# Context tail of a perceiver block: compact key-value matrices, attention in 32x64 tiles, two correction groups, last Gram split by column block

## Chip, cores, metric
The kernel runs on one core of one Trainium2 chip. The metric is the device time of one execution in microseconds (us), as the median of several executions. All data is 32-bit floating point at the borders of the kernel. An engine name below is one of TensorE (PE), VectorE (DVE), ScalarE (ACT), GpSimd (POOL) and SyncE (SP), which issues the transfers.

## What is computed
The reference is one perceiver layer: a linear cross attention to a context of 1601 rows for each of 8 batches, then a self attention and a gated mixture of experts. The change touches only the end of the first part:

```python
q = (decoder_seq @ Wq.T + bq).reshape(B, T_dec, N_HEADS, D_HEAD)   # 8, 64, 16, 32
k = (encoder_seq @ Wk.T + bk).reshape(B, T_enc, N_HEADS, D_HEAD)   # 8, 1601, 16, 32
v = (encoder_seq @ Wv.T + bv).reshape(B, T_enc, N_HEADS, D_HEAD)
kv = jnp.einsum('bthd,bthe->bhde', k, v)
att = jnp.einsum('bqhd,bhde->bqhe', q, kv) * scale
...
return layer_norm(att + decoder_seq, ln_gamma, ln_beta)
...
x = x + _L0_xattn_ref(ctx_1024, _layernorm(x, axis=-1), ...)
x = x + _L0_attn_ref(_layernorm(x, axis=-1), ...)
```

## The kernel before
There is no softmax in the cross attention, so each batch b needs only the Gram matrix G of its context (512x512), and from it one 32x32 matrix per head: KV = Wk G Wv^T, plus corrections of rank one for the two biases. The work is written out by hand, engine by engine, with semaphores between the engines; every engine runs its own list strictly in the order of the code.

For each batch TensorE sums the Gram matrix (`gram`, lines 936 to 960). Then `m_part(b, m)` makes block row m (128 rows) of M = G Wv^T in three products of halves (helper `three`, lines 367 to 369, 12 matmuls for each m), which ScalarE copies out (`m_copy`, line 656), and `kv_part(b)` (line 1008) makes the 16 head blocks. For the products G is held as a rounded part `gh` (made by ScalarE) and a remainder `gl` (made by VectorE).

The stretch that the change touches begins when the last Gram matrix (batch 7) is summed. There remain the M and KV of batch 6, the M and KV of batch 7, the corrections for batches 0 to 6, the attention of four tiles of 128 rows (two batches each), and the layer norms. In this stretch
- `group_corrections(n)` (lines 1093 and 1099) adds the bias terms to a group of batches: it copies their compact KV (128x128 each) into a PSUM bank by a product with the identity and adds 16 small products. The right operands are masked copies that ScalarE makes (`right_part`, line 716).
- `group_spread(n)` brings a group back to SBUF, spread from the compact 128 columns to a block-diagonal 128x512 matrix (VectorE line 1685, ScalarE line 734).
- `attend(i)` (line 1121) multiplies the queries of tile i with these matrices, in tiles of 128x64 of the array, into one bank.
- `part1_out(i)` (line 1700 and the four after it), `part1_residual(i)` (line 1714) and `norm_back(2, i)` (line 1473) on VectorE add the query's input to it, take two layer norms and give the rows `xn` of tile i. `transposes_1(i)` (line 1149) turns them on TensorE, and `xT_pair_high` and `xT_pair_low` (lines 755 and 1722) split them for `project_1`, the first product of the second part (lines 367 to 369, at 128x256).
- `kv_spread(7)` (line 1571) stands on VectorE behind `norm_back(2, 2)`; `attend(3)` waits for it, and `project_1` stands right behind `attend(3)`.
- `w_high(W_Q1)` on ScalarE (line 704) and `w_low(W_Q1)` on VectorE (line 1660) split the weight that `project_1` uses; the second waits for the first.
- `last_gh_high` and `last_gl_low` split the last Gram matrix, whose lower blocks still lie in PSUM after `last_g_transposes` (line 980).

```python
            group_spread(0)
            last_gl_low()
            part1_out(0)
            part1_residual(0)
            part1_out(1)
            norm_back(2, 0)
            part1_residual(1)
            part1_out(2)
            norm_back(2, 1)
            part1_residual(2)
            norm_back(2, 2)
            dve.wait_ge(xb_done, NT)
            kv_spread(B - 1)
            xT_pair_low(1, 0, range(KC))
            part1_out(3)
```

Of the kernel before, what the change touches and what calls it, by code (L numbers as in the profile page):

```python
# [34 lines left out]
def perceiver_block(nc, a, out):  # L35
# [25 lines left out]
    with ExitStack() as ctx:  # L61
# [230 lines left out]
        def att_bank(i):  # L292

            return bank[(5, 0, 3, 7)[i]]

# [17 lines left out]

        groups = ((0, 2), (2, 4), (4, 7))

        def group_bank(n):

            return bank[(1, 2, 4)[n]][:, 0:P * (groups[n][1] - groups[n][0])]

# [53 lines left out]
        def _(sp):  # L373
# [219 lines left out]
        def _(act):  # L593
# [116 lines left out]
            m_copy(B - 2, (1,))  # L710
            w_high(W_Q1, 0, 1)
            m_copy(B - 2, (2,))

# [3 lines left out]

            def last_gh_high():
                act.wait_ge(m_mm, (B - 1) * 4)
                act.wait_ge(gl_done, B - 1)  # L720
                act.wait_ge(g_add, 6 * B)
                act.activation(upper(ghf, 5 * P), upper(g32f, 5 * P), ACT.Copy).then_inc(gh_done, 1)
                act.activation(last_block(ghf), last_block(g32f), ACT.Copy).then_inc(gh_done, 1)
                act.wait_ge(gt_mm, 1)
                act.activation(lower(ghf), mir[:, 0:2, :].rearrange("p m n -> p (m n)")[:, 0:6 * P].rearrange("p (m n) -> p m n", m=3),
                               ACT.Copy).then_inc(gh_done, 1)

            def group_spread(n):

                act.wait_ge(r2_mm, n + 1)  # L730
                src = group_bank(n).rearrange("p (m d) -> p m d", d=D1)
                dst = kv[:, groups[n][0]:groups[n][1], :].rearrange("p b (c j d) -> p (b c) j d", j=4, d=D1)
                for j in range(4):
                    act.activation(dst[:, :, j, :], src, ACT.Copy, scale=headmask[:, D1 * j:D1 * j + 1]).then_inc(r2_act, 1)
# [12 lines left out]
            right_part(B - 1)  # L747
            m_copy(B - 1, (1,))
            w_high(W_OUT, 1, 1)
# [102 lines left out]
        def _(pe):  # L852
# [130 lines left out]
            def m_part(b, m, first):  # L983

                if first and m == 0:
                    pe.wait_ge(w_lo, 2)
                    pe.wait_ge(q_done, KC)
                if m == 0:
                    pe.wait_ge(gl_done, b + 1 if not isinstance(b, int) or b < B - 1 else B + 2)
                if not first and m == 0:  # L990
                    pe.wait_ge(kv_done, b)
# [8 lines left out]
            def kv_part(b, cs=range(KC)):  # L1000

                if cs.start == 0:
                    pe.wait_ge(m_done, b * 4 + 4)
                for c in cs:
                    for k in range(KC):
                        for j in range(4):
                            cols = slice(c * P + D1 * j, c * P + D1 * j + D1)
                            mm = pe.matmul(head_block(bank[6], c, j), wk[:, k, cols], mb[:, k, cols],  # L1008
                                           start=(k == 0), stop=(k == KC - 1))
                if cs.stop == KC:  # L1010
                    mm.then_inc(kv_mm, 1)

# [36 lines left out]
            with pe.Fori(2, B - 1) as b:  # L1049
                gram(b, False, lambda: kv_part(b - 2))  # L1050
                products_of(b - 1, False)
            gram(B - 1, False, lambda: kv_part(B - 3))

# [30 lines left out]
            def group_corrections(n):  # L1084

                first, end = groups[n]
                if n == 0:
                    pe.wait_ge(bk_near, 1)
                    pe.wait_ge(rk_near, 1)
                if n == 2:  # L1090
                    pe.wait_ge(gl_done, B + 2)
                pe.wait_ge(kv_done, end)
# [10 lines left out]
            def attend(i):  # L1103

                if i == 0:
                    pe.wait_ge(mir_mm, 1)
                    pe.wait_ge(g_add, 6 * B)
                if i == 1:
                    pe.wait_ge(rk_near, 1)
                    pe.wait_ge(right_near, 1)  # L1110
                if i == 0:
                    pe.wait_ge(r2_dve, 2)
                elif i < NT - 1:
                    pe.wait_ge(r2_act, 4 * i)
                else:
                    pe.wait_ge(kv_done, B)
                for c in range(KC):
                    for b in (2 * i, 2 * i + 1):
                        cols = slice(c * P, (c + 1) * P)
                        p0 = S * (b % 2)  # L1120
                        mm = pe.matmul(att_bank(i)[p0:p0 + S, cols], qT[:, c, b * S:(b + 1) * S], kv[:, b, cols],  # L1121
                                       start=True, stop=True)
                mm.then_inc(att_mm, 1)
# [52 lines left out]

            for m in range(2, KC):
                m_part(B - 1, m, False)
            last_kv_part()
# [279 lines left out]
        def _(dve):  # L1459
# [220 lines left out]
            def group_spread(n):  # L1680

                dve.wait_ge(r2_mm, n + 1)
                for b in range(groups[n][0], groups[n][1]):
                    m = b - groups[n][0]
                    dve.tensor_tensor(by_head_of(kv[:, b, :]), spread_heads(group_bank(n)[:, m * P:(m + 1) * P]), near_heads,
                                      ALU.mult).then_inc(r2_dve, 1)

            def last_gl_low():
                dve.wait_ge(gh_done, B + 1)
                dve.tensor_tensor(upper(glf, 5 * P), upper(g32f, 5 * P), upper(ghf, 5 * P).bitcast(F32), ALU.subtract).then_inc(gl_done, 1)  # L1690
                dve.tensor_tensor(last_block(glf), last_block(g32f), last_block(ghf).bitcast(F32), ALU.subtract).then_inc(gl_done, 1)
                dve.wait_ge(gh_done, B + 2)
                dve.tensor_tensor(lower(glf), mir[:, 0:2, :].rearrange("p m n -> p (m n)")[:, 0:6 * P].rearrange("p (m n) -> p m n", m=3),
                                  lower(ghf).bitcast(F32), ALU.subtract).then_inc(gl_done, 1)
# [29 lines left out]

            group_spread(0)
            last_gl_low()
            part1_out(0)
# [262 lines left out]
```

## Time and profile before
| | |
|---|---|
| median of 3 executions | 561.12 us (561.01 to 561.72) |
| profiled execution | 561.45 us, span 559.7 us |
| mean granted clock of TensorE | 0.997 of full speed |
| busy: PE, DVE, ACT, POOL | 546.4, 377.6, 283.6, 245.8 us |

The span runs from the first to the last instruction. A timeline row gives the start of an instruction (or of several alike, with their count), its duration, its engine and line, what it writes and reads, its shape, and in brackets how long the engine had been idle before it and what ended that. Matmuls overlap in the engine's pipeline, so the time that a block of them takes is read from its first start to the start of the next block. One fp32 matmul of the code is two in the trace.

### The profile page before, as it was taken

To read this page: it belongs to the slowest core of one execution; us is meant where nothing else is said; L and a number is where in the kernel's file an instruction comes from. 1 tells how busy PE (TensorE), PEld (TensorE's weight loads), DVE (VectorE), ACT (ScalarE), POOL (GpSimd) and SP (SyncE) were. 2 spreads that over 40 slices of the span, in tenths; PEclk is the share of its full clock that TensorE was granted. 3 is DMA by queue.
4 is the path that set the end of the run, shared out by engine and by line. 5 is a ranking of instruction groups with operands and counts; after the bars stand their busy time and mean duration, and the time that the engine had idled before them with its cause. 6 is when DMAs were issued, how large, how long until landed. Compare 5 with 4: busy or idle time off the path is not lost.

```text
span 559.7 us, 11752 instructions
## 1 busy us (share of the span) xinstructions
PE 546.4 (98%) x4873; PEld 466.9 (83%) x4875; DVE 377.6 (67%) x482; ACT 283.6 (51%) x486; POOL 245.8 (44%) x182
## 2 busy tenths in 40 slices
PE   9999969999999999999899999999999999999997
PEld 7988759898988989897679998978788888888886
DVE  4899488695977868684597477476584457867731
ACT  4687764886949496872742543424331213434220
POOL 2297989776766769677025001103345443000000
PEclk9999989999999999999999999999999999999999
DMA  8742562523432332305640004207733222899502
GB/s 309 255 142 82 211 188 77 185 77 114 148 101 94 133 123 75 114 1 185 165 171 4 10 8 147 76 2 189 198 122 105 75 81 81 207 249 212 150 0 76
DMA packets 31414, 69.13 MB, mean 123 GB/s; under 512 B 6928, under 2 KB 6928, under 8 KB 28432
## 3 DMA queue, kind: packets, MB, share of 16 engines
q1 hardware_dynamic: 31376, 68.58, 40.4%
q8 instruction: 29, 0.48, 0.4%
q14 instruction: 9, 0.07, 0.0%
HBM read 67.39 MB, written 1.18 MB: 123 GB/s over the span
## 4 chain that ended last, share of the span: by engine, by line
PE 84%; DVE 2%; issue 1%; POOL 1%; ACT 0%; POOLq 0%
PE ps L367 18%; PE ps L369 17%; PE ps L368 17%; PE ps L936 8%; PE ps L956 3%; PE ps L960 3%; PE ps L952 2%; PE ps L947 2%; PE ps L946 2%; PE ps L951 2%; PE ps L1008 2%; PE ps L1245 1%; PE ps L1228 1%; PE ps L1121 1%; PE ps L1158 1%
## 5 line engine op out<-in xcount | busy, mean ns | idle before, releaser
L533 POOL TENSOR_TENSOR psum_tmp<-psum_tmp,raw 128x512 f32<-128x512 f32 (+1 forms) x86 | 157.3, 1829 | 26.9 <-DVE lo L1491 18.6
L936 PE MATMUL ps<-hi 128*128 128x256 f32 (+1 forms) x384 | 120.6, 316 | 6.4 <-DVE lo L1491 6.4
L936 PEld LDWEIGHTS ps<-hi 128*128 128x128 f32 x384 | 73.2, 191 | 8.7 <-issue 5.7
L367 PE MATMUL ps<-hi,gh 128*128 128x512 f32 x192 | 75.5, 393 | 0.0
L369 PE MATMUL ps<-hi,gl 128*128 128x512 f32 x192 | 74.8, 390 | 0.0
L368 PE MATMUL ps<-lo,gh 128*128 128x512 f32 x192 | 74.7, 389 | 0.0
L586 POOL TENSOR_TENSOR sx<-sx,raw 128x512 f32<-128x512 f32 x32 | 41.1, 1291 | 76.4 <-DVE raw L1883 76.2
L631 ACT ACTIVATE kv<-par 32x320 f32<-32x320 f32 x112 | 52.7, 470 | 40.3 <-DVE par L1539 39.0
L823 ACT ACTIVATE hi<-raw 128x2048 fp32r<-128x2048 f32 x14 | 26.9, 1918 | 88.6 <-PE ps L369 79.3
L1491 DVE TENSOR_TENSOR lo<-raw,hi 128x2048 fp32r<-128x2048 f32 (+1 forms) x28 | 70.1, 2503 | 0.3
L367 PE MATMUL ps<-wvh,gh 128*128 128x512 f32 x128 | 50.9, 398 | 0.0
L369 PE MATMUL ps<-wvh,gl 128*128 128x512 f32 x128 | 49.9, 390 | 0.0
L368 PE MATMUL ps<-wvl,gh 128*128 128x512 f32 x128 | 49.9, 390 | 0.0
L511 POOL TENSOR_TENSOR rstd<-vareps,expo 128x1 f32<-128x1 f32 x16 | 11.1, 695 | 84.1 <-DVE vareps L1467 84.1
L607 ACT ACTIVATE hi<-raw 128x2048 fp32r<-128x2048 f32 (+1 forms) x28 | 42.7, 1540 | 10.2 <-DMA raw<-in_ctx 10.0
L1889 DVE TENSOR_TENSOR lo<-raw,hi 128x2048 fp32r<-128x2048 f32 x15 | 34.4, 2291 | 18.0 <-ACT hi L823 17.9
L369 PEld LDWEIGHTS ps<-hi,gl 128*128 128x128 f32 x192 | 36.0, 188 | 7.5
L640 ACT ACTIVATE g<-par 32x192 f32<-32x192 f32 x112 | 40.6, 363 | 3.3 <-DVE par L1558 2.1
L367 PEld LDWEIGHTS ps<-hi,gh 128*128 128x128 f32 x192 | 36.0, 188 | 7.5
L368 PEld LDWEIGHTS ps<-lo,gh 128*128 128x128 f32 x192 | 36.1, 188 | 7.3
L956 PE MATMUL ps<-lo,hi 128*128 128x512 f32 x104 | 41.5, 399 | 0.0
L960 PE MATMUL ps<-lo,hi 128*128 128x512 f32 x104 | 41.2, 396 | 0.0
(231 smaller groups left out, 1187.9 us busy)
## 6 DMA issues: line engine op xcount, KB each, us to landing
raw<-in_ctx SPq DMA_DIRECT2D x22, 1024.0 KB, 5.3
raw<-in_ve SPq DMA_DIRECT2D x8, 1024.0 KB, 6.1
raw<-in_oe SPq DMA_DIRECT2D x8, 1024.0 KB, 6.6
wk<-gm_rows SPq DMA_DIRECT2D x8, 512.0 KB, 9.2
g<-gm_rows SPq DMA_DIRECT2D x8, 512.0 KB, 10.8
raw<-in_ctx SPq DMA_DIRECT2D x16, 128.0 KB, 4.2
cb<-in_ctx SPq DMA_DIRECT2D x8, 256.0 KB, 3.2
xres<-in_x SPq DMA_DIRECT2D x1, 1024.0 KB, 9.6
```

The source lines that it names most:

```text
L367: pe.matmul(dst, wh, xh, start=first, stop=False)
L368: pe.matmul(dst, wh, xl, start=False, stop=False)
L369: return pe.matmul(dst, wl, xh, start=False, stop=last)
L533: pool.tensor_tensor(psum_tmp[0:k, :], psum_tmp[0:k, :] if n else rows(order[0]), rows(t)[0:k, :], ALU.add).then_inc(ctx_sum, 1)
L586: pool.tensor_tensor(v, v, tmp[:, i % 2, :].rearrange("p (h k) -> p h k", k=D2), ALU.add).then_inc(v_added, 1)
L607: act.activation(hi[:, r, :], ctx_rows(b, c), ACT.Copy).then_inc(ctx_hi, 1)
L631: ins = act.activation(turned[dst, :, :, src], flipped[src, :, dst].rearrange("p (r s) n -> p r s n", s=2), ACT.Copy)
L640: ins = act.activation(low_pairs(dst)[:, :, :, src], upflip[src, :, :, dst], ACT.Copy)
L936: pe.matmul(dst, hi[:, t, cols], x, start=start and opens, stop=t == CH * ROWS - 1 and closes, skip_group_check=True)
L956: pe.matmul(mir[:, 0, :], w, lb, start=start, stop=stop, skip_group_check=True)
L960: mm = pe.matmul(mir[:, 1, :], w, lb, start=start, stop=stop, skip_group_check=True)
L1491: dve.tensor_tensor(lo[rows, r, :], ctx_rows(b, c)[rows, :, :], hi[rows, r, :].bitcast(F32), ALU.subtract).then_inc(ctx_lo, 1)
```

## The change
The key-value matrices of batches 0 to 5 stay compact. The corrections are made for two groups (batches 0 to 3 and 4 to 6) in place of three. Tiles 0 to 2 are attended head by head in tiles of 32x64 of the array, into four banks, one for each row group. The lower blocks of the last Gram matrix are first copied to SBUF, and its `gh` and `gl` are then made by column block, four pieces each. The program order changes with it on TensorE, ScalarE and VectorE: `last_g_transposes` and `m_part(7, 0)` come before the corrections, `attend(0)` and `attend(1)` stand together behind `kv_part(6)`, and the two steps that split W_Q1 come later.

```diff
-            return bank[(5, 0, 3, 7)[i]]
+            return bank[7] if i == NT - 1 else ps[:, 2:6, i * P:(i + 1) * P].rearrange("p j (c d) -> p c j d", d=D1)
+
+        def kv_bank(b):
+
+            return bank[0][:, 3 * P:4 * P] if isinstance(b, int) and b == B - 2 else bank[6][:, 0:P]
...
-        groups = ((0, 2), (2, 4), (4, 7))
+        groups = ((0, 4), (4, 7))
...
-            sp.wait_ge(r2_mm, 2)
+            sp.wait_ge(r2_mm, 1)
             sp.dma_start(raw[:, half(1), :], blocks(a["owT"])).then_inc(ld_w[1], 16)
-            sp.wait_ge(gl_done, B + 2)
+            sp.wait_ge(gl_done, B + 3)
             sp.dma_start(g32[:, :, :], blocks(a["vw"])).then_inc(ld_qv, 16)
...
@@ ScalarE
             m_copy(B - 2, (1,))
-            w_high(W_Q1, 0, 1)
-            m_copy(B - 2, (2,))
...
+            def last_lower_blocks():
+                act.wait_ge(gt_mm, 1)
+                act.activation(lower(g32f), mir[:, 0:2, :].rearrange("p m n -> p (m n)")[:, 0:6 * P].rearrange("p (m n) -> p m n", m=3),
+                               ACT.Copy).then_inc(lower_done, 1)
+
+            def last_gh_high(m):
+                act.wait_ge(m_mm, (B - 2) * 4 + m + 1)
...
+                act.activation(gh[:, :, of_tile(m)], g32[:, :, of_tile(m)], ACT.Copy).then_inc(gh_done, 1)
...
+            last_lower_blocks()
+            last_gh_high(0)
+            last_gh_high(1)
+            m_copy(B - 2, (2,))
             for b in range(4):
                 right_part(b)
             m_copy(B - 2, (3,))
-            last_gh_high()
-            group_spread(1)
+            last_gh_high(2)
+            last_gh_high(3)
             act.wait_ge(kv_mm, B - 1)
-            act.activation(kv[:, B - 2, 0:P], bank[6][:, 0:P], ACT.Copy).then_inc(kv_done, 1)
+            act.activation(kv[:, B - 2, 0:P], kv_bank(B - 2), ACT.Copy).then_inc(kv_done, 1)
+            m_copy(B - 1, (0,))
             for b in range(4, 7):
                 right_part(b)
-            m_copy(B - 1, (0,))
-            group_spread(2)
+            w_high(W_Q1, 0, 1)
+            m_copy(B - 1, (1,))
+            group_copy(1)
             right_part(B - 1)
-            m_copy(B - 1, (1,))
             w_high(W_OUT, 1, 1)
...
@@ TensorE
             def attend(i):
 
                 if i == 0:
-                    pe.wait_ge(mir_mm, 1)
-                    pe.wait_ge(g_add, 6 * B)
...
+                    pe.wait_ge(lower_done, B)
+                    pe.wait_ge(r2_dve, 1)
+                if i == 2:
+                    pe.wait_ge(r2_act, 1)
+                    pe.wait_ge(y_done, 2)
+                if i == NT - 1:
+                    pe.wait_ge(r2_act, 5)
                     pe.wait_ge(kv_done, B)
...
+                        for j in range(4):
+                            row = slice(D1 * j, D1 * j + D1)
+                            mm = pe.matmul(att_bank(i)[p0:p0 + S, c, j, :], qT[row, c, b * S:(b + 1) * S], kv[row, b, D1 * c:D1 * c + D1],
+                                           start=True, stop=True, skip_group_check=True)
...
             sum_rows()
+            last_g_transposes()
             m_part(B - 2, 2, False)
             m_part(B - 2, 3, False)
+            m_part(B - 1, 0, False)
             group_corrections(0)
-            last_g_transposes()
+            kv_part(B - 2, kv_bank(B - 2))
+            attend(0)
+            attend(1)
+            m_part(B - 1, 1, False)
             group_corrections(1)
-            kv_part(B - 2)
-            attend(0)
-            m_part(B - 1, 0, False)
-            attend(1)
-            group_corrections(2)
-            m_part(B - 1, 1, False)
+            m_part(B - 1, 2, False)
             attend(2)
+            m_part(B - 1, 3, False)
 
             def transposes_1(i):
 
+                if i == 0:
+                    pe.wait_ge(y_done, NT - 1)
                 pe.wait_ge(s_norm[2], i + 1)
...
@@ VectorE
-            w_low(W_Q1, 0)
...
             def part1_out(i):
 
                 dve.wait_ge(s_norm[0], i + 1)
-                dve.wait_ge(att_mm, i + 1)
-                dve.tensor_tensor(xn[:, i, :], xn[:, i, :], att_bank(i)[:, :], ALU.add).then_inc(y_done, 1)
+                dve.wait_ge(att_mm, max(i + 1, 2))
+                dve.tensor_tensor(by_head_of(xn[:, i, :]), by_head_of(xn[:, i, :]), att_bank(i) if i < NT - 1 else by_head_of(att_bank(i)),
+                                  ALU.add).then_inc(y_done, 1)
...
-            group_spread(0)
-            last_gl_low()
+            for m in range(KC):
+                last_gl_low(m)
+            group_copy(0)
+            w_low(W_Q1, 0)
             part1_out(0)
```

Three places show how the lists of the engines differ. The line numbers of the changed kernel are 4 to 13 higher for the same code. First ScalarE, before, from the split of W_Q1 (line 704, reads `raw`, writes `hi`) to the right operands of batches 4 to 6; `mb` is a copy of M, `gh` the rounded Gram matrix:

```order
L704 ACTIVATE hi<-raw 128x2048 [waits ld_w0]
L656 ACTIVATE mb<-ps 128x512 [waits m_mm]
L716 ACTIVATE raw<-raw,batch_of 128x512 [waits right_near] x4
L656 ACTIVATE mb<-ps 128x512 [waits m_mm]
L722 ACTIVATE gh<-g 128x3x384 [waits g_add,gl_done,m_mm]
L723 ACTIVATE gh<-g 128x128
L725 ACTIVATE gh<-ps 128x3x256 [waits gt_mm]
L734 ACTIVATE kv<-ps,headmask 128x8x32 [waits r2_mm]
L734 ACTIVATE kv<-ps,headmask 128x8x32 x3
L742 ACTIVATE kv<-ps 128x128 [waits kv_mm]
L716 ACTIVATE raw<-raw,batch_of 128x512 [waits right_near] x3
```

The same stretch of the changed kernel, where the split of W_Q1 is line 708:

```order
L722 ACTIVATE g<-ps 128x3x256 [waits gt_mm]
L730 ACTIVATE gh<-g 128x4x128 [waits g_add,lower_done,gl_done,m_mm] x2
L660 ACTIVATE mb<-ps 128x512 [waits m_mm]
L718 ACTIVATE raw<-raw,batch_of 128x512 [waits right_near] x4
L660 ACTIVATE mb<-ps 128x512 [waits m_mm]
L730 ACTIVATE gh<-g 128x4x128 [waits g_add,lower_done,gl_done,m_mm] x2
L752 ACTIVATE kv<-ps 128x128 [waits kv_mm]
L660 ACTIVATE mb<-ps 128x512 [waits m_mm]
L718 ACTIVATE raw<-raw,batch_of 128x512 [waits right_near] x3
L708 ACTIVATE hi<-raw 128x2048 [waits ld_w0]
```

The split of W_Q1 has moved from the head of the list to its end, behind the copy of KV of batch 6 (which waits for `kv_mm`), a copy of M and three right operands.

Second VectorE, before, from the last mask of the right operands (line 1677) to the first instruction of `part1_out(0)` (line 1700):

```order
L1677 TENSOR_TENSOR raw<-raw,hm 128x512 [waits pick_done,rv_sum]
L1660 TENSOR_TENSOR lo<-raw,hi 128x2048 [waits w_hi]
L1685 TENSOR_TENSOR kv<-ps,headmask 128x512 [waits r2_mm]
L1685 TENSOR_TENSOR kv<-ps,headmask 128x512
L1690 TENSOR_TENSOR gl<-g,gh 128x3x384 [waits gh_done]
L1691 TENSOR_TENSOR gl<-g,gh 128x128
L1693 TENSOR_TENSOR gl<-ps,gh 128x3x256 [waits gh_done]
L1700 TENSOR_TENSOR xn<-xn,ps 128x512 [waits att_mm,s_norm0]
```

And in the changed kernel, where these are lines 1690 and 1705, and the remainder of W_Q1 is line 1673:

```order
L1690 TENSOR_TENSOR raw<-raw,hm 128x512 [waits pick_done,rv_sum]
L1699 TENSOR_TENSOR gl<-g,gh 128x4x128 [waits gh_done] x4
L1695 COPY kv<-ps 128x4x128 [waits r2_mm]
L1673 TENSOR_TENSOR lo<-raw,hi 128x2048 [waits w_hi]
L1705 TENSOR_TENSOR xn<-xn,ps 128x512 [waits att_mm,s_norm0]
```

The remainder of W_Q1, which waits for ScalarE's half, now stands directly ahead of `part1_out(0)`.

Third TensorE, before, from the corrections of the first group (line 1093) to `attend(0)` (line 1121); line 980 is `last_g_transposes`, line 1008 `kv_part(6)`:

```order
L1093 MATMUL ps<-kv,ident 128x256 [waits kv_done,rk_near,bk_near]
L1099 MATMUL ps<-raw 32x2x32 [waits rb_done]
L1099 MATMUL ps<-raw 32x2x32 x15
L980 MATMUL ps<-ident,g 128x128 [waits g_add]
L980 MATMUL ps<-ident,g 128x128 x5
L1093 MATMUL ps<-kv,ident 128x256 [waits kv_done]
...
L1008 MATMUL ps<-mb,wk 32x32 [waits m_done]
L1008 MATMUL ps<-mb,wk 32x32 x63
L1121 MATMUL ps<-kv,qT 64x128 [waits r2_dve,g_add,mir_mm]
L1121 MATMUL ps<-kv,qT 64x128 x7
```

In the changed kernel, from the transposes (line 991, now ahead of `m_part(6, 2)`) to the two attended tiles; the row of line 371 with `gl_done` opens `m_part(7, 0)`:

```order
L991 MATMUL ps<-ident,g 128x128 [waits g_add]
...
L371 MATMUL ps<-wvh,gh 128x512 [waits m_done,gl_done]
...
L1102 MATMUL ps<-kv,ident 128x512 [waits kv_done,rk_near,bk_near]
L1108 MATMUL ps<-raw 32x4x32 [waits rb_done]
L1108 MATMUL ps<-raw 32x4x32 x15
L1020 MATMUL ps<-mb,wk 32x32 [waits m_done]
L1020 MATMUL ps<-mb,wk 32x32 x63
L1133 MATMUL ps<-kv,qT 64x32 [waits r2_dve,lower_done]
L1133 MATMUL ps<-kv,qT 64x32 x63
```

`kv_part(6)` stands behind `m_part(7, 0)` and one larger group of corrections, and the 64 matmuls of tiles 0 and 1 follow it.

## Rows read from the trace of the kernel before

**Rows 1.** The page, part 1: busy time of each engine over the span.
```profile
PE 546.4 (98%) x4873; PEld 466.9 (83%) x4875; DVE 377.6 (67%) x482; ACT 283.6 (51%) x486; POOL 245.8 (44%) x182
```

**Rows 2.** Timeline of TensorE, from sum_rows to project_1.
```profile
267.13 0.50 PE L367 MATMUL ps<-wvh,gh 128*128 128x512 f32 x1
...
270.03 0.39 PE L367 MATMUL ps<-wvh,gh 128*128 128x512 f32 x1
...
272.76 0.60 PE L1093 MATMUL ps<-kv,ident 128*128 128x256 f32 x2
...
273.87 0.87 PE L980 MATMUL ps<-ident,g 128*128 128x128 f32 x6
274.58 0.60 PE L1093 MATMUL ps<-kv,ident 128*128 128x256 f32 x2
...
275.58 1.30 PE L1008 MATMUL ps<-mb,wk 128*32 128x32 f32 x128
276.81 0.76 PE L1121 MATMUL ps<-kv,qT 128*64 128x128 f32 x9
279.08 0.66 PE L1121 MATMUL ps<-kv,qT 128*64 128x128 f32 x7 [1.51 <-issue]
...
283.65 0.91 PE L1093 MATMUL ps<-kv,ident 128*128 128x384 f32 x2
...
285.29 0.50 PE L367 MATMUL ps<-wvh,gh 128*128 128x512 f32 x1
...
296.48 1.09 PE L1149 MATMUL ps<-ident,xn 128*128 128x128 f32 x8
297.51 1.09 PE L1121 MATMUL ps<-kv,qT 128*64 128x128 f32 x16
298.53 0.39 PE L367 MATMUL ps<-gh,hi 128*128 128x256 f32 x1
```

**Rows 3.** Timeline of ScalarE, same stretch.
```profile
265.39 0.60 ACT L656 ACTIVATE mb<-ps 128x512 f32<-128x512 f32 x1 [3.50 <-PE ps L369]
265.88 1.90 ACT L704 ACTIVATE hi<-raw 128x2048 fp32r<-128x2048 f32 x1
...
277.27 0.29 ACT L742 ACTIVATE kv<-ps 128x128 f32<-128x128 f32 x1
277.43 1.97 ACT L716 ACTIVATE raw<-raw,batch_of 128x512 f32<-128x512 f32 x3
```

**Rows 4.** Timeline of VectorE, same stretch.
```profile
269.32 2.29 DVE L1660 TENSOR_TENSOR lo<-raw,hi 128x2048 fp32r<-128x2048 f32 x1
...
279.85 0.69 DVE L1700 TENSOR_TENSOR xn<-xn,ps 128x512 f32<-128x512 f32 x1 [2.22 <-PE ps L1121]
...
284.62 0.69 DVE L1700 TENSOR_TENSOR xn<-xn,ps 128x512 f32<-128x512 f32 x1
...
289.45 0.69 DVE L1700 TENSOR_TENSOR xn<-xn,ps 128x512 f32<-128x512 f32 x1
...
291.84 0.54 DVE L1473 TENSOR_SCALAR xn<-xres,mv,rstd 128x512 f32<-128x512 f32 x1
...
295.01 1.51 DVE L1473 TENSOR_SCALAR xn<-xres,mv,rstd 128x512 f32<-128x512 f32 x1 [0.66 <-POOL rstd L511]
296.66 0.69 DVE L1571 TENSOR_TENSOR kv<-ps,headmask 128x512 f32<-128x512 f32 x1
297.70 1.42 DVE L1722 TENSOR_TENSOR gl<-ps,gh 128x256 fp32r<-128x256 f32 x4 [0.35 <-ACT gh L755]
```

**Rows 5.** Timeline of TensorE where it idled longest.
```profile
75.07 0.68 PE L936 MATMUL ps<-hi 128*128 128x384 f32 x1 [5.26 <-DVE lo L1491]
```

**Rows 6.** Windows there; after busy times: granted clock, DMA share, GB/s.
```profile
74.50:75.00 0.50, 0.00 (x0) 0.00 (x0) 0.50 (x2) 0.00 (x0) 0.50 (x1) 0.67 0.71 270
...
78.00:78.50 0.50, 0.50 (x41) 0.36 (x43) 0.50 (x2) 0.50 (x2) 0.34 (x2) 0.91 0.00 0
```

**Rows 7.** Timeline of TensorE, products in 32x64 tiles of the second part.
```profile
314.01 1.63 PE L1214 MATMUL ps<-qT 32*64 32x64 f32 x128
```

More of the change, by code:

```diff
@@ L312, in right_of @@
             return raw[:, 4 + b, :] if b < B - 1 else psum_tmp[:, :]
-        groups = ((0, 2), (2, 4), (4, 7))
+        groups = ((0, 4), (4, 7))
         def group_bank(n):
-            return bank[(1, 2, 4)[n]][:, 0:P * (groups[n][1] - groups[n][0])]
+            return bank[(1, 0)[n]][:, 0:P * (groups[n][1] - groups[n][0])]
         def by_tile(t):
@@ L987, in m_part @@
                     pe.wait_ge(q_done, KC)
[L988 to L991, printed above, removed]
+                if isinstance(b, int) and b == B - 1:
+                    pe.wait_ge(gl_done, B + m)
+                elif m == 0:
+                    pe.wait_ge(gl_done, b + 1)
+                    if not first:
+                        pe.wait_ge(kv_done, b)
                 if not (first and m < 2):
@@ L998, in m_part, with kv_part @@
                 mm.then_inc(m_mm, 1)
[L1000 to L1004, printed above, removed]
+            def kv_part(b, dst):
+                pe.wait_ge(m_done, b * 4 + 4)
+                for c in range(KC):
                     for k in range(KC):
@@ L1007, in kv_part @@
                             cols = slice(c * P + D1 * j, c * P + D1 * j + D1)
[L1008 to L1011, printed above, removed]
+                            mm = pe.matmul(head_block(dst, c, j), wk[:, k, cols], mb[:, k, cols],
+                                           start=(k == 0), stop=(k == KC - 1), skip_group_check=True)
+                mm.then_inc(kv_mm, 1)
             def last_kv_part():
@@ L1049, in _ @@
             with pe.Fori(2, B - 1) as b:
-                gram(b, False, lambda: kv_part(b - 2))
+                gram(b, False, lambda: kv_part(b - 2, bank[6]))
                 products_of(b - 1, False)
-            gram(B - 1, False, lambda: kv_part(B - 3))
+            gram(B - 1, False, lambda: kv_part(B - 3, bank[6]))
             def row_sums():
@@ L1089, in group_corrections @@
                     pe.wait_ge(rk_near, 1)
-                if n == 2:
-                    pe.wait_ge(gl_done, B + 2)
                 pe.wait_ge(kv_done, end)
@@ L1120, in attend @@
                         p0 = S * (b % 2)
-                        mm = pe.matmul(att_bank(i)[p0:p0 + S, cols], qT[:, c, b * S:(b + 1) * S], kv[:, b, cols],
-                                       start=True, stop=True)
+                        if i == NT - 1:
+                            mm = pe.matmul(att_bank(i)[p0:p0 + S, cols], qT[:, c, b * S:(b + 1) * S], kv[:, b, cols],
+                                           start=True, stop=True)
+                            continue
+                        for j in range(4):
+                            row = slice(D1 * j, D1 * j + D1)
+                            mm = pe.matmul(att_bank(i)[p0:p0 + S, c, j, :], qT[row, c, b * S:(b + 1) * S], kv[row, b, D1 * c:D1 * c + D1],
+                                           start=True, stop=True, skip_group_check=True)
                 mm.then_inc(att_mm, 1)
@@ L1175, in project_1 @@
                         mm.then_inc(q_mm, 1)
-            for m in range(2, KC):
-                m_part(B - 1, m, False)
             last_kv_part()
@@ L1677, in _, with group_copy, last_gl_low @@
             dve.tensor_tensor(by_tile(right), by_tile(right), near4(slice(0, P)), ALU.mult).then_inc(right_near, 1)
-            w_low(W_Q1, 0)
-            def group_spread(n):
+            def group_copy(n):
                 dve.wait_ge(r2_mm, n + 1)
[L1683 to L1694, printed above, removed]
+                dve.tensor_copy(kv[:, groups[n][0]:groups[n][1], 0:P], group_bank(n).rearrange("p (m d) -> p m d", d=P)).then_inc(r2_dve, 1)
+            def last_gl_low(m):
+                dve.wait_ge(gh_done, B + m)
+                dve.tensor_tensor(gl[:, :, of_tile(m)], g32[:, :, of_tile(m)], gh[:, :, of_tile(m)].bitcast(F32), ALU.subtract).then_inc(gl_done, 1)
             def part1_out(i):
                 dve.wait_ge(s_norm[0], i + 1)
-                dve.wait_ge(att_mm, i + 1)
-                dve.tensor_tensor(xn[:, i, :], xn[:, i, :], att_bank(i)[:, :], ALU.add).then_inc(y_done, 1)
+                dve.wait_ge(att_mm, max(i + 1, 2))
+                dve.tensor_tensor(by_head_of(xn[:, i, :]), by_head_of(xn[:, i, :]), att_bank(i) if i < NT - 1 else by_head_of(att_bank(i)),
+                                  ALU.add).then_inc(y_done, 1)
                 dve.wait_ge(y_done, i + 1)
```

26 lines of the change are left out of this document (7 added, 19 removed).

## Prediction
> **What bounds the kernel now.** I read the page's busy times first: TensorE is busy for 546.4 of 559.7 us [rows 1], so a change pays only where it takes work or waits off TensorE, and costs wherever it makes TensorE wait. Then its timeline in the touched stretch: one gap of 1.51 us stands out, in the middle of `attend(0)`, with no other engine as its releaser [rows 2]. Then the timelines of the three engines side by side from 267 to 299 us. TensorE has no other gap there: `project_1` starts at 298.53, straight behind `attend(3)` (297.51), which follows the transposes (296.48) [rows 2]. The reader should see how narrow that is. VectorE starts `part1_out(0)` at 279.85, has `part1_out(1)` and `(2)` at 284.62 and 289.45, `norm_back(2, 1)` at 291.84, and `kv_spread(7)` from 296.66 to 297.35, 0.16 us before `attend(3)` [rows 4]. Of these 17.5 us the largest idle time is 0.66, for one of GpSimd's small powers ahead of 295.01; the list is dense. So two chains end together at `project_1`: TensorE's work, and VectorE's list from `part1_out(0)` on. The start of `part1_out(0)` decides for the second; I call it T0, now 279.85.
>
> **TensorE's own sum.** Attention of a tile takes 1.02 us (297.51 to 298.53, 16 matmuls in the trace) [rows 2]. After, tiles 0 to 2 have 64 each, of 32 columns in 32x64 tiles. No row has just this; the nearest is 128 of 64 columns in the same tiles in 1.63 us, 12.7 ns each [rows 7], which gives 0.81 us as the upper bound; 128 of 32 columns in 128x32 tiles start in 1.23 us (275.58 to 276.81) [rows 2], 9.6 ns each, which gives 0.61. I take 0.7: 3 x 0.3 = 0.9 us less. Corrections: a group of two takes 1.11 us (272.76 to 273.87) or 1.00 (274.58 to 275.58), one of three 1.64 (283.65 to 285.29) [rows 2]. One batch more costs 0.53, so a group of four takes 2.17; together 3.75 before, 3.81 after, no gain. The gap of 1.51 may go or stay. So TensorE alone would gain 0.9 to 2.4 us. On ScalarE and VectorE the spreads become cheaper copies and the Gram pieces stay as large in sum; both lie before T0 and beside matmuls, so they count only through T0.
>
> **T0 after the change.** Step by step from 267.13, where TensorE has finished `sum_rows` in either kernel (nothing ahead of it is changed on its path):
> - `last_g_transposes` 0.71 (273.87 to 274.58), `m_part(6, 2)` 2.90 and `m_part(6, 3)` 2.73 (267.13, 270.03, 272.76), `m_part(7, 0)` 2.73 more, corrections of the group of four 2.17, `kv_part(6)` 1.23 [rows 2]. That is 12.47, so `kv_mm` comes at 279.6, or 279.65 with the end of the last matmul, against 276.9 before. `m_part(7, 0)` starts at 273.5 and needs only the first column block of `gh` and `gl`. From the transposes at 267.84, ScalarE copies 768 and 512 columns (under the 1.90 of 2048) [rows 3] and VectorE makes a remainder of 512 (under 2.29) [rows 4]: done by 272.0 at the latest, so `m_part(6, 2)` and `(6, 3)` cover it; without them `m_part(7, 0)` would wait up to 4.2 us.
> - ScalarE stands at its copy of KV of batch 6 and waits for it. Behind it: the copy itself 0.16 to the next start (277.27 to 277.43), a copy of M 0.49 (265.39 to 265.88), three right operands 1.9 (of 1.97), then `w_high(W_Q1)` 1.90 [rows 3]. Sum 4.45: done at 284.1. Before, this last step ended at 267.8, under `sum_rows`.
> - VectorE has nothing to do between its copy of the group (278.4 + at most 0.69, 279.1) and this. `w_low(W_Q1)` takes 2.29 [rows 4]. T0 = 286.4.
> - `part1_out(0)` also waits for tiles 0 and 1: 279.6 + 2 x 0.7 = 281.0, or 282.5 with a gap as now. That is covered by 4 us or more.
>
> So T0 moves from 279.85 to 286.4, by 6.55 us. That is the main term. Queued behind the waiting `w_low` are all of `part1_out`, `part1_residual`, `norm_back`, `kv_spread(7)` and `xT_pair_low`; GpSimd's small powers wait with them.
>
> **What TensorE does with it.** It has the work up to `attend(2)` done at about 281.0 + 2.9 + 1.64 + 2.8 = 288.3 (289.8 with the gap). The copy of the second group on ScalarE, needed by then, comes after `w_high(W_Q1)` and `m_copy(7, 1)`, at about 286, in time. But `attend(2)` now waits for `y_done` 2, which is T0 + 5.46 (284.62 + 0.69 - 279.85) [rows 4] = 291.9: a new wait of 2 to 3.5 us. Behind it stand `m_part(7, 3)`, the last KV product and the transposes. They end about 297.2. `transposes_1(0)` needs `y_done` 3, T0 + 10.3 = 296.7, no wait; `transposes_1(1)` needs `norm_back(2, 1)`, T0 + 12.5 = 298.9, a wait of 1.2. They end at 299.5. `attend(3)` needs `kv_spread(7)`, T0 + 17.5 = 303.9: a wait of 4.4. Then 1.02, and `project_1` starts at 304.95 where it started at 298.53, 6.4 us later. `xT_pair_low` no longer waits for ScalarE (0.35 before) [rows 4] and gives nothing more, for TensorE waits at `attend(3)`. All that TensorE saved in its own work lies ahead of these waits and is lost in them. Behind `project_1` TensorE has no slack to give it back [rows 1]. The loads are not in the way: owT is issued at the end of the first corrections (278.4), 2.8 us later than now and used at 287; wq2 is issued at T0, and its split comes after the second part's first products.
>
> **Sum.** 559.7 + 6.4 = 566.1 us of span. The profiled execution took 561.45 with this span, 0.33 above the median, which is 0.06%. On the median: 561.12 + 6.4 = 567.5.
>
> **The clock.** TensorE idled for 5.26 us before 75.07 [rows 5], and its granted clock, full until then, went to half (2.4 to 1.2 GHz) at about 74.7, some 5 us into the idle stretch, and came back near 78.05 [rows 6]. So 3.0 us of work ran at half speed and cost 1.5 us. The gap of 1.51 us cost none. The new wait of 4.4 us, with another of 1.2 and two short blocks of transposes ahead of it, lies between these, nearer to the first. If the clock falls in it, about 1.5 us is lost in `project_1`, which is TensorE's own work. If it falls in the wait ahead of `attend(2)`, the loss lies in the slack and costs nothing. The Trainium skill, "TensorE: Matmul & The Clock Gate", Part 1, states that an idle array is put back to half its clock and regains it only after sustained work; the row at 75.07 agrees, and by that rule the sum would be 6.4 + 1.5 = 7.9.
>
> **Rivals.**
> - *Clock falls as well*: 6.4 + 1.5, 569.0 us. For it the row at 74.5, against it that 4.4 is less than 5.
> - *The gap in issue comes ahead of `kv_mm`.* The gap stands behind a dense run: 128 matmuls in 1.23 us. After, the dense run is longer (128 and then 128). Counted in matmuls from the loop's end, the place of the present gap falls in the first quarter of the new attention, behind `kv_mm`, where 4 us cover it. If it fell inside `kv_part(6)`, T0 moves by 1.5 more: 569.0. The Trainium skill, "Runtime: NRT & Kernel Launch", Instruction fetch mechanics, calls the crossing of an instruction block mostly hidden; the 1.51 us above is a gap without another engine as releaser, and by that rule no term changes.
> - *VectorE's late start costs less*: the wait of 0.66 for GpSimd shrinks, or the group of four takes only 1.64 and the copies are quicker. Floor: T0 cannot be before tiles 0 and 1 are attended, 281.0, which is +1.2 us. Between: 562.3 to 566.
> - *Faster*: TensorE's own sum decides, 0.9 to 2.4 us less, 558.7 to 560.2. The place is `attend(3)`: it would need `kv_spread(7)` done no later than about 297, so T0 at 279.6 or earlier, or a list of VectorE that is some 7 us shorter. For it speaks only the 1.51 us gap; against it the 0.16 us between `kv_spread(7)` and `attend(3)`, and the order of lines 708 and 1673.
> - *No change*: the two cancel, by the same doubtful shortening.
>
> **How the numbers follow.** Forecast (+6.4, own range 566.3 to 568.4): 0.50. Clock as well: 0.28. Gap ahead of `kv_mm`, or both (up to 570.5): 0.08. Less: 0.08. Within 0.2% (1.1 us, about what a measurement of this kernel tells from none): 0.03. Faster: 0.03. The bounds of the terms: corrections 1.64 instead of 2.17 give -0.5, GpSimd's waits shrinking -0.6, which makes 566.3; the upper end takes in the clock and 0.6 of pipeline ends and handovers, 569.7.
>
> **What the profile after would show.** VectorE idle for about 4.5 to 5 us ahead of line 1673, ended by ScalarE's line 708; that starts near 282.2. Line 1705 first at 286.4. TensorE idle before `attend(2)` for 2 to 3.5 us, before the second tile's transposes for about 1, before `attend(3)` for about 4.4. `project_1` at 305. A granted clock of half for some 3 us behind 303, or none. I would be wrong if line 1705 starts before 284, if TensorE doesn't wait at `attend(3)`, or if VectorE's list from there is much shorter than 17.5 us (the reads of four banks could make it longer).

## The result, and the profile after
The changed kernel takes 570.6 us (570.01 to 571.33), the kernel before 561.42 in the same comparison: ratio 1.0157, 95% interval 1.0142 to 1.0172, so 8.8 us slower by the ratio. The profiled execution has a span of 568.3 us against 559.7, 8.6 more. Slower was forecast, and so was the place; the size was not (6.4 us, 567.5, with an upper end of 569.7).

The waits of TensorE in the kernel after: engine, line, waited for what, us in total, times, longest.

```profile
PE ps L947 <- DVE lo L1504: 6.4, 2, 5.2
PE ps L1128 <- DVE kv L1584: 3.2, 1, 3.2
PE ps L1133 <- issue: 2.0, 1, 2.0
PE ps L1039 <- issue: 2.0, 1, 2.0
...
PE ps L1108 <- issue: 1.1, 1, 1.1
```

The first row was there before. The second is new: `attend(3)` waits for `kv_spread(7)`, which [rows 4] had done 0.16 us ahead of it. The other three (lines 1133, 1039 and 1108) are gaps that no engine releases; in this stretch of the kernel before there was one, of 1.51 us [rows 2].

The timeline of VectorE and ScalarE after:

```profile
280.16 0.28 ACT L752 ACTIVATE kv<-ps 128x128 f32<-128x128 f32 x1 [3.87 <-PE ps L1020]
280.33 0.59 ACT L660 ACTIVATE mb<-ps 128x512 f32<-128x512 f32 x1
280.81 1.94 ACT L718 ACTIVATE raw<-raw,batch_of 128x512 f32<-128x512 f32 x3
282.65 1.91 ACT L708 ACTIVATE hi<-raw 128x2048 fp32r<-128x2048 f32 x1
```

```profile
284.58 2.29 DVE L1673 TENSOR_TENSOR lo<-raw,hi 128x2048 fp32r<-128x2048 f32 x1 [4.82 <-ACT hi L708]
286.79 0.68 DVE L1705 TENSOR_TENSOR xn<-xn,ps 128x512 f32<-128x512 f32 x1
...
303.33 0.68 DVE L1584 TENSOR_TENSOR kv<-ps,headmask 128x512 f32<-128x512 f32 x1
```

This is the forecast chain, link by link: ScalarE idles until KV of batch 6 is there (line 1020 is `kv_part`), makes five copies (the KV, a copy of M, three right operands), splits W_Q1 (line 708), VectorE has idled 4.82 us for it, subtracts (line 1673), and only then starts `part1_out(0)` (line 1705) at 286.79. In [rows 4] that stood at 279.85.

The timeline of TensorE after, with the matmuls of `m_part` left out:

```profile
276.97 1.02 PE L1102 MATMUL ps<-kv,ident 128*128 128x512 f32 x2
277.92 1.08 PE L1108 MATMUL ps<-raw 128*32 128x128 f32 x32
278.82 1.30 PE L1020 MATMUL ps<-mb,wk 128*32 128x32 f32 x128
280.05 0.45 PE L1133 MATMUL ps<-kv,qT 32*64 32x32 f32 x31
282.50 1.18 PE L1133 MATMUL ps<-kv,qT 32*64 32x32 f32 x97 [2.00 <-issue]
...
292.39 0.85 PE L1133 MATMUL ps<-kv,qT 32*64 32x32 f32 x64
...
299.65 0.28 PE L1039 MATMUL ps<-psum_tmp,raw 128*32 128x32 f32 x10 [1.97 <-issue]
299.86 1.09 PE L1164 MATMUL ps<-ident,xn 128*128 128x128 f32 x8
304.16 1.97 PE L1128 MATMUL ps<-kv,qT 128*64 128x128 f32 x16 [3.20 <-DVE kv L1584]
306.06 0.58 PE L371 MATMUL ps<-gh,hi 128*128 128x256 f32 x1
```

`attend(3)` starts at 304.16 (297.51 before) and now takes 1.90 us to the next start instead of 1.02. The granted clock says why. Windows of one microsecond after; the third last number is the clock:

```profile
302.00:303.00 1.00, 0.00 (x0) 0.00 (x0) 1.00 (x1) 0.00 (x0) 1.00 (x1) 0.57 0.00 0
...
308.00:309.00 1.00, 1.00 (x7) 1.00 (x7) 0.72 (x2) 0.00 (x0) 0.86 (x1) 0.52 0.00 0
```

It fell to half at about 302.1, after 2 us of a gap (297.7 to 299.7), one microsecond of transposes and then idleness from 300.9, and stayed there until 309. All of `attend(3)` and the first part of `project_1` ran at 1.2 GHz. The mean granted clock is 0.988 in all four executions of the changed kernel. In the 34 timed executions of the kernel before beside the experiments of the next section it was 0.990 to 0.997; the one of [rows 5] and [rows 6], with a single stretch of 3.4 us at half speed, has 0.997.

### The profile page after: what moved, and what is told of

It is laid out like the page before. It is cut to its first block, busy times and chain, and to the rows that moved or that the text cites. A ratio compares the mean times of both kernels' runs of the same rounds, so it can differ in the third digit from the quotient of the medians.

```text
span 568.3 us, 11982 instructions
## 1 busy us (share of the span) xinstructions
PE 547.8 (96%) x4983; PEld 468.4 (82%) x4985; DVE 377.2 (66%) x482; ACT 281.8 (50%) x485; POOL 245.3 (43%) x182
## 4 chain that ended last, share of the span: by engine, by line
PE 82%; DVE 2%; issue 1%; ACT 1%; POOL 1%; POOLq 0%; DVEq 0%
PE ps L371 18%; PE ps L372 17%; PE ps L373 17%; PE ps L947 8%; PE ps L967 3%; PE ps L971 3%; PE ps L963 2%; PE ps L958 2%; PE ps L957 2%; PE ps L962 2%; PE ps L1020 2%; PE ps L1258 1%; PE ps L1241 1%; DVE stats L1476 1%; PE ps L1173 1%
## 5 line engine op out<-in xcount | busy, mean ns | idle before, releaser
L967 PE MATMUL ps<-lo,hi 128*128 128x512 f32 x104 | 41.5, 399 | 0.0
L1891 DVE TENSOR_TENSOR raw<-ps,sx 128x512 f32<-128x512 f32 x32 | 22.0, 689 | 29.1 <-PE ps L373 29.1
```

Of the source, the lines that this page charges most:

```text
L967: pe.matmul(mir[:, 0, :], w, lb, start=start, stop=stop, skip_group_check=True)
```

## The experiments
Each runs beside the kernel before on the same chip, so differences are given as ratios to it, and "us over before" is worked out from the ratio; "before" was 562.47 us for the first four and 561.67 for the next three, 562.07 for the last. Every kernel here computes the whole layer; order, groups and waits differ (e3 adds matmuls whose result is not used).

**e1: the changed kernel, the split of W_Q1 early again.**

```diff
+            w_high(W_Q1, 0, 1)
             last_lower_blocks()
...
                 right_part(b)
-            w_high(W_Q1, 0, 1)
             m_copy(B - 1, (1,))
...
+            w_low(W_Q1, 0)
             for m in range(KC):
                 last_gl_low(m)
             group_copy(0)
-            w_low(W_Q1, 0)
             part1_out(0)
```

> The changed kernel with the split of W_Q1 put back where it was (ScalarE's half ahead of last_lower_blocks, VectorE's half ahead of last_gl_low). Theory A (the split between kv_mm and part1_out(0) is the cost): part1_out(0) starts when tiles 0 and 1 are attended, about 283.7 us instead of 286.8, attend(3) 3.1 us earlier, the clock does not fall in front of it (another 2.2 us): 570.6 - 5.3 = 565.3 us; what is left over 561.4 is the gaps in issue and the order on TensorE. Rival B (the 32x64 attention, its number of instructions and their gaps in issue are the cost): within 1 us of 570.6.

Measured: 566.47 us, ratio 1.0062 (1.0043 to 1.0081), 3.5 us over before instead of 8.8 (by the medians as they stand it is 4.1 us faster than the changed kernel, by the ratios 5.3). The timeline of VectorE in e1:

```profile
283.59 0.69 DVE L1705 TENSOR_TENSOR xn<-xn,ps 128x512 f32<-128x512 f32 x1 [4.53 <-PE ps L1133]
```

`part1_out(0)` starts at 283.59, 3.2 us earlier, and what it waits for is now the attention itself (line 1133). Of these 3.2 us 0.7 is there already where `sum_rows` ends (267.38, and 268.07 in the changed kernel). Theory A holds for this part of the loss. The clock did fall again in the profiled execution, though, from 301.3 on, which I had excluded, and a first time from 284.2 to 287.7, behind a gap of 2.50 us in the attention.

**e2: the kernel before, the split of W_Q1 late.**

```diff
             m_copy(B - 2, (1,))
-            w_high(W_Q1, 0, 1)
...
             for b in range(4, 7):
                 right_part(b)
+            w_high(W_Q1, 0, 1)
             m_copy(B - 1, (0,))
...
-            w_low(W_Q1, 0)
...
             last_gl_low()
+            w_low(W_Q1, 0)
             part1_out(0)
```

> The kernel before with one part of the change alone: the split of W_Q1 late (ScalarE's half behind the right operands of batches 4 to 6, VectorE's half directly ahead of part1_out(0)). Theory A: kv_mm at 276.9 is now 2.7 us earlier than in the changed kernel, so part1_out(0) starts at 283.5 instead of 279.85: +3.6 us, 565.1 us, and up to 2.2 more where the clock falls in the wait ahead of attend(3). Rival B: no change, 561.4.

Measured: 566.43 us, ratio 1.0076 (1.0049 to 1.0103), 4.3 us over. TensorE in e2:

```profile
301.09 1.80 PE L1121 MATMUL ps<-kv,qT 128*64 128x128 f32 x16 [3.03 <-DVE kv L1571]
```

With nothing else changed, moving two instructions gives the wait ahead of `attend(3)` (3.03 us) and a slow `attend(3)` (1.73 to the next start, at 302.82). In e2 the transposes follow the last KV product without a gap, and yet the clock falls, at about 301.7:

```profile
301.00:302.00 1.00, 0.91 (x10) 0.91 (x12) 1.00 (x5) 0.00 (x0) 1.00 (x2) 0.66 0.00 0
...
304.00:305.00 1.00, 1.00 (x8) 1.00 (x7) 0.93 (x4) 0.00 (x0) 0.10 (x1) 0.64 0.00 0
```

So an idle time of 3.03 us in one piece was enough. `part1_out(0)` started at 283.82, where 283.5 was expected. Rival B said no change.

**e3: the changed kernel with filling work in the wait.**

```diff
             transposes_1(1)
+            for _ in range(14):
+                pe.matmul(bank[3][:, :], blank[:, 0:P], blank[:, :], start=True, stop=True)
             attend(NT - 1)
```

> The changed kernel with 14 added bf16 matmuls of 512 columns on a blank operand into a free bank, between transposes_1(1) and attend(3), where TensorE waits 3.2 us for kv_spread(7). They do nothing but keep TensorE at work. Theory A with the clock as second term (attend(3) and the first project_1 ran at 1.2 GHz from 304.2 to 309.0): the clock stays at full speed there, -2.2 us, 568.4. Rival: the clock costs nothing there because VectorE's list sets the end: 570.6 or slightly more.

Measured: 568.66 us, ratio 1.0099 (1.0077 to 1.0121), 5.6 over before, so some 3 us under the changed kernel. But the profiled execution, the slowest of the four, shows that the clock was not kept. TensorE in e3:

```profile
301.38 4.87 PE L1196 MATMUL ps<-blank 128*128 128x512 bf16 x14
306.18 1.09 PE L1128 MATMUL ps<-kv,qT 128*64 128x128 f32 x16
```

The clock fell at 301.7, 0.3 us into the filler, so 14 matmuls took 4.8 us, and `attend(3)` came 2 us later but at full speed (1.09). The filler moved the loss rather than removing it in this execution. It shows that the fall does not need the long wait: the gap of 2.1 us and the transposes ahead of it were enough, and the lower median agrees with a cost of the clock of 2 to 3 us; its exact size is not settled by e3. The clock also stood at half from 284.7 to 288.1 in e3, behind the gap in the attention (1.92 us), which it did not in the changed kernel's profiled execution.

**e4: e1 with attend(0) and attend(1) ahead of kv_part(6).**

```diff
             group_corrections(0)
-            kv_part(B - 2, kv_bank(B - 2))
             attend(0)
             attend(1)
+            kv_part(B - 2, kv_bank(B - 2))
             m_part(B - 1, 1, False)
```

> e1 with attend(0) and attend(1) ahead of kv_part(6) on TensorE. part1_out(0) starts about 281.2 instead of 283.7 by theory A. If VectorE's list still set the end, another 2.5 us would be gained (562.8). If TensorE's own work with its gaps in issue (2.0, 1.1 and 2.0 us in the changed kernel) sets it by now, it stays at e1's time, about 565, and the gaps are what is left of the loss.

Measured: 570.62 us, ratio 1.0149 (1.0124 to 1.0173): as slow as the changed kernel, 5 us over e1, which neither branch had expected. TensorE in e4:

```profile
280.77 1.48 PE L1133 MATMUL ps<-kv,qT 32*64 32x32 f32 x128 [0.91 <-DVE kv L1695]
282.17 0.45 PE L1020 MATMUL ps<-mb,wk 128*32 128x32 f32 x31
287.84 1.55 PE L1020 MATMUL ps<-mb,wk 128*32 128x32 f32 x97 [5.22 <-issue]
```

The gap is at the same place in the instruction stream as in the changed kernel: behind one run of 128 small matmuls and 31 more. There the 31 were attention and here they are `kv_part`, so it belongs to the stream and not to the operation. And it is 5.22 us long instead of 2.00. Behind it the clock stood at half from 285.0 to 291.9, `attend(2)` started only at 297.83, and VectorE waited 6.78 us for it; that is where e4 lost what the early start of its attention had gained. (`attend(3)` itself ran at full clock.) On the queue of instruction blocks (30 blocks with 0.49 MB in all in the changed kernel, so 16 KB each) one block falls into the window 279.5 to 280 in the changed kernel, and in e4 none before 285.0 to 285.5, where the rows of the two DMA queues are:

```profile
q1 hardware_dynamic: 94, 0.19, 97.0%
q8 instruction: 1, 0.02, 11.7%
```

The queues carry three loads of 1 MB by then. The last three of SyncE's rows in e4, with the time of issue first:

```profile
279.92 0.38 SPq L443 DMA_DIRECT2D raw<-in_owT  x1
280.35 0.51 SPq L445 DMA_DIRECT2D g<-in_vw  x1
280.90 0.51 SPq L447 DMA_DIRECT2D raw<-in_wq  x1
```

**e5: e4 with these loads later.**

```diff
-            sp.wait_ge(r2_mm, 1)
+            sp.wait_ge(att_mm, 2)
             sp.dma_start(raw[:, half(1), :], blocks(a["owT"])).then_inc(ld_w[1], 16)
```

> e4 with the loads of owT and vw issued when tiles 0 and 1 are attended (att_mm 2) instead of at the end of the first corrections. In e4 TensorE stood still for 5.2 us after the 31st matmul of kv_part(6), the same place in its instruction stream as the 2.0 us gap of the changed kernel, and its block of instructions (16 KB) came at 285.2 only, behind these two loads of 1 MB. Theory C (TensorE waits for its instructions, and they wait behind the loads): the block comes at about 281.5, the gap shrinks to 2 us, TensorE is 3.2 us earlier, and with the shorter gap the clock need not fall (up to 1.9 more): 8.3 us over before becomes 3.2 to 5.1, so 565.7 to 567.6 against 562.5. Rival: the gap is a property of the order (a drain of the array between tile shapes): no change, +8.3.

Measured: 566.94 us, ratio 1.008 (1.0058 to 1.0101), 4.5 over before where e4 was 8.4. TensorE in e5:

```profile
280.87 0.45 PE L1020 MATMUL ps<-mb,wk 128*32 128x32 f32 x31
283.35 1.32 PE L1020 MATMUL ps<-mb,wk 128*32 128x32 f32 x97 [2.02 <-issue]
```

The gap is 2.02 us at the same matmul. The first of the loads is issued at 280.97, 0.1 us behind the start of `kv_part(6)`, where in e4 it was 2.25 us ahead of it (279.92 and 282.17), and the instruction block comes in the window 280.5 to 281, ahead of the loads. This pair shows that the length of the gap follows the time at which the loads are issued, as theory C said: 2.3 to 3.0 us pass from the block's transfer to the next matmul (in the changed kernel, e4 and e5; 2.8 to 3.3 in e1), and big loads issued ahead of the block push it back. That TensorE waits for instructions is read from this order of events; the profile names no releaser. Not all of the time between the two kernels is the gap: of 3.3 us between their profiled executions 1.3 is there already where `sum_rows` ends (268.93 and 267.63), and in e5 the clock fell twice, from 283.8 and from 300.9 on, for 3.4 us each.

**e7 and e8: dense runs apart, then the loads later as well.** e7 is e1 with this order on TensorE (ScalarE's and VectorE's lists follow it); e8 also lets the loads of owT and vw wait for `kv_mm` 7.

```diff
-            m_part(B - 1, 0, False)
             group_corrections(0)
-            kv_part(B - 2, kv_bank(B - 2))
             attend(0)
             attend(1)
+            m_part(B - 1, 0, False)
+            kv_part(B - 2, kv_bank(B - 2))
             m_part(B - 1, 1, False)
             group_corrections(1)
             m_part(B - 1, 2, False)
             attend(2)
```

> The changed kernel with the split of W_Q1 early (as e1), and TensorE's order such that an m_part stands between every two dense runs of small matmuls: group_corrections(0), attend(0), attend(1), m_part(7,0), kv_part(6), m_part(7,1), group_corrections(1), m_part(7,2), attend(2), m_part(7,3); ScalarE and VectorE follow this order. Theories A and C: part1_out(0) starts near 278, before it started in the kernel before; the loads of owT and vw still start at the end of the first corrections, so the next block of instructions comes late and a gap of about 2 us stays in kv_part(6): 561.5 to 564 against 562.5 of before. Rival B (the 32x64 form itself costs): still 3 us or more over before.

> e7 with the loads of owT and vw issued after kv_part(6) (kv_mm 7). Theory C: the block of instructions comes in time, no gap in kv_part(6); 1 to 2 us less than e7 and at or below the kernel before: 560.5 to 562.5 against 562.5. If loads don't matter for the gaps, e8 equals e7.

Measured: e7 564.98, ratio 1.006 (1.004 to 1.008); e8 564.62, ratio 1.0049 (1.0034 to 1.0064). That is 3.4 and 2.8 us over before, where at most 1.5 and 0 were expected, and e8 is only 0.4 us under e7, where 1 to 2 were. For e7 it is also what rival B had forecast, 3 us or more; the times of e7 and e8 can't tell it from the theories, only their traces and e9 can. In e8 `kv_part(6)` runs without a gap, as expected (128 matmuls from 281.33, `group_corrections(1)` from 285.40 behind an `m_part`), and in e7 with one of 1.16. The block of instructions comes in the window 278.0 to 278.5 in e8 and 280.0 to 280.5 in e7, where the first load is issued at 275.75 instead of 282.66, with the same order on TensorE: the second pair for theory C. `part1_out(0)` starts at 278.18 and 278.52, earlier than in the kernel before. The gain is lost two steps further. TensorE in e7, and VectorE and TensorE in e8:

```profile
282.61 1.03 PE L1019 MATMUL ps<-mb,wk 128*32 128x32 f32 x97 [1.16 <-issue]
```

```profile
290.83 0.69 DVE L1704 TENSOR_TENSOR xn<-xn,ps 128x512 f32<-128x512 f32 x1 [2.64 <-PE ps L1132]
```

```profile
297.25 0.28 PE L1038 MATMUL ps<-psum_tmp,raw 128*32 128x32 f32 x10 [2.10 <-issue]
```

Tile 2 now waits for `attend(2)`, because its group of corrections holds batch 6 as well and so must follow `kv_part(6)`; and the last KV product again has a gap without a releaser. In e8 the clock stood at half from 298.6 to 302.0, over `attend(3)`. e7's six executions go with the clock: three with a mean granted clock of 0.997 took 563.70 to 564.15 us, three with 0.990 to 0.994 took 565.80 to 566.46. By the mean clock (0.003 to 0.007 of 562 us, doubled: an estimate) that is 3.4 to 8 us more at half speed for 1.7 to 2.8 us. It is a correlation over executions of one kernel, and not a test of one fall.

**e9: three groups, transposes earlier.** This is e8 with groups of batches 0 to 3, 4 and 5, and 6. The diff shows the groups and TensorE's order; ScalarE's and VectorE's lists follow them.

```diff
-        groups = ((0, 4), (4, 7))
+        groups = ((0, 4), (4, 6), (6, 7))
...
             kv_part(B - 2, kv_bank(B - 2))
+            group_corrections(1)
             m_part(B - 1, 1, False)
-            group_corrections(1)
-            m_part(B - 1, 2, False)
             attend(2)
-            m_part(B - 1, 3, False)
+            group_corrections(2)
+            m_part(B - 1, 2, False)
...
-            last_kv_part()
+            pe.wait_ge(r2_act, 5)
             transposes_1(0)
             transposes_1(1)
+            m_part(B - 1, 3, False)
+            last_kv_part()
             attend(NT - 1)
```

> e8 with three groups again (batches 0 to 3, 4 and 5, 6), so that attend(2) needs no KV of batch 6 and comes right after m_part(7,1), and with the transposes of tiles 0 and 1 ahead of m_part(7,3) and last_kv_part. In e8 part1_out(0) started at 278.5, earlier than before, but part1_out(2) then waited 2.6 us for attend(2), and TensorE stood still 2.1 us in last_kv_part for its instructions. By theories A and C: part1_out(2) no longer waits; 42 more matmuls ahead of last_kv_part move the border of the instruction block so that m_part(7,3) lies between the last two borders, and the gap in last_kv_part goes; attend(3) at about 297, which is 1 to 2 us under the kernel before: 560.2 to 561.5 against 561.7 of before. If the gap in last_kv_part stays, level with before or 1 us over. Rival B (the 32x64 form costs): over before by 2 us or more.

Measured: 562.82 us, ratio 1.0011 (1.0002 to 1.002), level with the kernel before; 1 to 2 us under it was expected. The wait for `attend(2)` shrank to 0.72 us and the gap in the last KV product went, as expected from moving the border of the instruction blocks (several things change at once in e9, so the reason is argued), but one of 0.96 came in `group_corrections(1)`, and `attend(3)` waits 0.95 for `kv_spread(7)`, which waits for the last KV product. Rival B had forecast 2 us or more over before. So the compact matrices and the 32x64 attention, in this order of the work, cost 0.1 to 1.1 us by the interval, and they gain nothing measurable. No kernel here beats the one before.

## Why the prediction was right and wrong
*What bounds the stretch: right.* VectorE's list from `part1_out(0)` to `attend(3)` took 17.37 us (286.79 to 304.16) where 17.66 was measured before and 17.5 used. e1 and e2 show both directions of it: the split of W_Q1 between `kv_mm` and `part1_out(0)` is worth 5.3 us taken out of the changed kernel and 4.3 put into the kernel before, by the ratios and with what the clock did in either.

*T0: right in mechanism, 0.55 us too large.* The profiled execution of the changed kernel is 0.94 us late already at 268.07, where `sum_rows` ends (267.13 before), so `part1_out(0)` moved by 286.79 - 0.94 - 279.85 = 6.0 us, not 6.55. The term that was mis-sized most is the group of four: 1.85 us (276.97 to 278.82), forecast 2.17 by adding a batch at 0.53. The other 0.23 is spread: 0.17 in the transposes and the three `m_part`s (8.90 for 9.07), the rest in the split.

*TensorE's waits: half right.* The forecast wait of 2 to 3.5 us at `attend(2)` did not come; `attend(2)` (292.39) started 0.14 behind the end of `y_done` 2 (291.56 + 0.69). The place was filled by gaps: I had taken one, like the present 1.51, and there were three, 2.00, 1.06 and 1.97 us. They lay in slack, as forecast for the first, and cost nothing directly. The third came 1 us of transposes ahead of the wait in which the clock fell; whether the fall needed it is open, for e2 has a fall without such a gap. And the wait at `attend(3)` was only 3.20 instead of 4.4.

*The clock: the step that failed.* The sum put its cost at nothing. It was a rival at 0.28 and 1.5 us, argued against because 4.4 us of idleness is less than the 5 of [rows 5]. The clock fell after less: a gap of 1.97 us, eight transposes, and 1.2 us into the wait; in e2 a wait of 3.03 was enough. One row of a fall behind 5 us was an example and no lower limit. The clock also stayed low twice as long as in [rows 6], 6.8 us for 3.4, and 2.0 us of that were spent waiting; in the stretch of 6.9 us at half in e4 TensorE waited as well, for 2.8 us. Why it stays low longer there is not shown. Its price by rows at the two levels: `attend(3)` 1.90 for 1.02, the first 12 products of `project_1` 2.73 (306.06 to 308.79) for 1.53, the transposes 0.44 for 0.36, together 2.2 us. That it fell is shown by the rows. The mean of 0.988 in all four executions says that each had some 13.6 us at half (an estimate, 0.012 of 568.3 us, doubled), as much as the two stretches of the profiled one together. What exactly would keep the clock up is not settled, since e3's filler came too late.

*What was not in the sum.* The 0.94 us ahead of the touched code: 0.40 is already there at the idle stretch of [rows 5] (75.47 after), and the rest is the same fall of the clock as in [rows 6], which in the changed kernel's execution lasted from 73.4 to 80.3. The KV product behind the idle stretch took 1.83 us to the next start (80.37) for 1.22 (79.36), first before and then after:

```profile
78.14 1.30 PE L1008 MATMUL ps<-mb,wk 128*32 128x32 f32 x128
```

```profile
78.54 1.90 PE L1020 MATMUL ps<-mb,wk 128*32 128x32 f32 x128
```

It lies in code that the change doesn't touch, and executions of the kernel before vary in it too (spans of 559.5 to 560.5 us at a clock of 0.997, 559.7 to 561.5 at 0.994). The long fall is not tied to the new program: e2, which is the kernel before up to there, has it (72.6 to 79.4), and e3 and e7, which are the changed kernel up to there, have the short one. Whether the whole 0.94 us is chance stays open: `sum_rows` ends at 267.4 to 268.9 in the eight traces of the changed kernel and its variants, and at 267.1 and 267.5 in those of the kernel before and of e2.

The account: 0.94 + 6.0 - 0.29 (17.37 for 17.66) + 2.2 = 8.85 us, against 8.6 of span. On the path that was forecast, 6.4 us, the measured part is 5.7.

*The other rivals.* Faster and no change are out. The gap ahead of `kv_mm` did not happen: it fell behind it, after 31 of the 128 matmuls, in the first quarter of the new attention as counted. "By that rule no term changes" held for T0 in this kernel and would have misled in e4, where the wait for instructions was 5.22 us and on the path. Cheaper attention: 64 matmuls took 0.78 us (292.39 to 293.17), near the upper bound (0.81) and not the 0.7 taken, hidden either way.

## What to carry to other kernels
An operation that is off the path where it stands (a weight split under other work) becomes the path when it is put between a late product and a chain of an engine that has no slack; before moving one, write down the start of that chain and add up what now precedes it, DMA and all. Count idle time and nearly idle time together when asking whether the clock will hold: small transposes between two waits did not hold it, and one fall seen behind a long idle time says nothing about shorter ones. Put slower work between runs of hundreds of tiny matmuls, and issue no large loads just ahead of them: so arranged, `kv_part(6)` ran without a gap in e8.

## What was unexpected of the hardware
TensorE stood still for 1.0 to 2.5 us behind dense runs of small matmuls, at the same place of its instruction stream whatever the operation there was, and for 5.22 us when the first of three loads of 1 MB had been issued 2.25 us ahead of the run; issued 0.1 us behind its start they left a gap of 2.02 us (e4, e5). Each time a block of 16 KB of instructions had arrived 2.3 to 2.9 us ahead of the next matmul. The granted clock fell in e3 and in the changed kernel when TensorE had been idle for no more than 2.1 us in one piece, and it stayed at half for 6.8 to 6.9 us where 2 us or more of that time were idle (the changed kernel, e4), against 3.4 in [rows 6], where work followed within 0.4 us.
